# A graph-network layer on one core: VectorE adds chunk sums half by half, one-hots in between

## The reference

```python
msg = node_feat[src] + edge_feat                              # 400000 x 64
agg = jax.ops.segment_sum(msg, dst, num_segments=12500)       # sum of the messages of each node
h = jax.nn.relu(agg @ W1 + b1)                                # 64 -> 128
x = _layernorm(x + (h @ W2 + b2), axis=-1)                    # 128 -> 64
```

## Time and profile before

| | |
|---|---|
| median of 3 runs | 1467.95 us |
| profiled execution | 1467.16 us |
| its span, first to last instruction | 1465.4 us |
| mean granted TensorE clock | 0.906 |
| TensorE busy | 1223.0 us, 83% |
| VectorE busy | 1217.6 us, 83% |
| GpSimd busy | 967.6 us, 66% |
| ScalarE busy | 751.7 us, 51% |

### The profile page before, as it was taken

How to read it: one execution, slowest core, us unless ns; L and a number is a source line. 1 busy time by engine, 2 the same in 40 slices (tenths; PEclk the granted TensorE clock), 3 DMA queues, 4 the chain that set the end, 5 groups by cost and what they waited for, 6 DMA issues and landing times.

```text
span 1465.4 us, 47112 instructions
## 1 busy us (share of the span) xinstructions
PE 1223.0 (83%) x18748; PEld 1107.5 (76%) x18749; DVE 1217.6 (83%) x2696; ACT 751.7 (51%) x941; POOL 967.6 (66%) x1043
## 2 busy tenths in 40 slices
PE   1457878888888899888989899999999999999873
PEld 1356777776778888887878889888888888898642
DVE  5499888898988898989998888888889899887333
ACT  3734322233445455554455666666666666665252
POOL 6767777777676677777767667676666766674132
PEclk8566698899998999999999999999999999999975
DMA  6724444444443444444443434444333444332132
GB/s 166 177 77 126 114 128 117 113 128 121 110 120 104 117 114 120 112 123 109 105 127 105 119 102 107 117 108 110 108 104 103 123 113 111 101 100 64 33 76 67
DMA packets 157980, 161.09 MB, mean 110 GB/s; under 512 B 52803, under 2 KB 141955, under 8 KB 157427
## 3 DMA queue, kind: packets, MB, share of 16 engines
q1 hardware_dynamic: 126149, 123.61, 28.6%
q0 software_dynamic: 31616, 34.50, 12.4%
HBM read 153.06 MB, written 4.93 MB: 108 GB/s over the span
## 4 chain that ended last, share of the span: by engine, by line
PE 44%; DVE 28%; issue 17%; DVEq 5%; ACT 3%; DMA 2%; POOL 1%; POOLq 0%; SPq 0%
PE sums_ps L1175 20%; PE counted_ps L1158 12%; DVE oh_key L953 11%; PE chunk_ps L1140 10%; DVE oh_lo L949 8%; DVEq L907 3%; ACT counts L741 3%; DVE lists L918 2%; DVE onehot L893 2%; DMA lists<-in_dst 1%; DVEq L918 1%; POOL x_parts L658 1%; DVE less_b L843 1%; DMA edge_records<-counts 1%; PE turn_ps L1186 1%
## 5 line engine op out<-in xcount | busy, mean ns | idle before, releaser
L617 POOL DMA_INDIRECT xmsg<-in_x,idx_t x925 | 888.4, 960 | 292.4 <-issue 275.0
L741 ACT CAST counts<-counted_ps 128x784 bf16<-128x784 f32 (+2 forms) x728 | 618.3, 865 | 500.8 <-PE counted_ps L1158 494.3
L1158 PE MATMUL counted_ps<-oh_key,oh_lo 128*128 128x98 bf16 (+1 forms) x5264 | 579.4, 232 | 143.6 <-DVE oh_key L953 109.5
L1175 PE MATMUL sums_ps<-x_parts,counts 128*128 128x193 bf16 (+3 forms) x4900 | 629.0, 254 | 0.3
L1158 PEld LDWEIGHTS counted_ps<-oh_key,oh_lo 128*128 128x128 bf16 x5264 | 381.8, 103 | 204.8 <-DVE oh_key L953 149.9
L949 DVE TENSOR_TENSOR oh_lo<-chunk_ps,tables 128x768 bf16<-128x768 f16 (+3 forms) x622 | 444.6, 715 | 94.6 <-PE counted_ps L1158 57.8
L953 DVE TENSOR_TENSOR oh_key<-chunk_ps,tables 128x1176 bf16<-128x1176 f16 (+2 forms) x622 | 459.5, 739 | 0.0
L1175 PEld LDWEIGHTS sums_ps<-x_parts,counts 128*128 128x128 bf16 (+3 forms) x4900 | 455.8, 118 | 4.6 <-issue 3.1
L1140 PE MATMUL chunk_ps<-onehot,cmsg 128*64 128x16 f32 (+4 forms) x4400 | 167.3, 222 | 6.3 <-DVE lists L918 5.3
L1140 PEld LDWEIGHTS chunk_ps<-onehot,cmsg 128*64 128x64 f32 x4400 | 153.6, 147 | 22.6 <-issue 9.5
L918 DVE TENSOR_TENSOR lists<-lists,chunk_ps 64x48 f32 (+6 forms) x625 | 113.8, 182 | 30.5 <-PE chunk_ps L1140 8.4
(11 more groups left out here) (104 smaller groups left out, 459.6 us busy)
## 6 DMA issues: line engine op xcount, KB each, us to landing
cmsg<-in_edge_attr SPq DMA_DIRECT2D x440, 160.0 KB
gmsg<-in_edge_attr SPq DMA_DIRECT2D x185, 160.0 KB
xmsg<-in_x,idx_t POOLq DMA_INDIRECT x925
x_parts<-in_x SPq DMA_DIRECT2D x12, 256.0 KB, 3.2
out_nodes<-x_parts SPq DMA_DIRECT2D x12, 256.0 KB, 2.6
edge_records<-counts SPq DMA_DIRECT2D x1, 1500.0 KB
lists<-in_src SPq DMA_DIRECT2D x1, 1400.0 KB
lists<-in_dst SPq DMA_DIRECT2D x1, 1400.0 KB
```

The lines of the kernel that those rows point to most:

```text
L617: pool.indirect_dma_start(xmsg[:, at * D:(at + 1) * D], None, x, bass.IndirectOffsetOnAxis(ap=idx_t[:, of:of + 1], axis=0)).then_inc(gathe ...
L741: nc.scalar.copy(to.rearrange("p h (m n) -> p h m n", m=m), ps.rearrange("p m (n h) -> p h m n", h=HI)).then_inc(unit_kept, 1)
L1158: mm = nc.tensor.matmul(unit_ps[u][:, col:col + slot.key_cols], oh_lo[s % RING][:, n * P:(n + 1) * P], oh_key[s % RING][:, n * slot.key_co ...
L1175: mm = nc.tensor.matmul(sums_ps[0:n, 0:XC], counts[b % 2][:, h * P:h * P + n], x_parts[:, h * XC:(h + 1) * XC], start=(h == 0), stop=(h == ...
```

## The change

The four adds of a visit are reordered, and a pair's one-hots go between two adds of one half. With places p0 to p3 of a visit, VectorE issued before: add p0 (half 0), p1 (half 1), p2 (half 0), p3 (half 1), one-hots A, one-hots B, register load. It now issues: add p0 (half 0), one-hots A, add p2 (half 0), add p1 (half 1), one-hots B, add p3 (half 1), register load. `ADDED` is numbered in the new order. `LAG` is 4, so the `range` steps are what they were.

```diff
+        def in_halves(places):
+
+            return places[0::2] + places[1::2]
+
         ADDED = {}
         half_of = lambda key: key[1] % 2 if key[0] == "chunk" else 0
         for s in range(NS + 1):
-            for place, _, _ in JOBS_AT[s]:
-                if place >= LAG:
-                    ADDED["chunk", place - LAG] = len(ADDED) + 1
+            for q in range(0, len(JOBS_AT[s]), LAG):
+                for place in in_halves([place for place, _, _ in JOBS_AT[s][q:q + LAG]]):
+                    if place >= LAG:
+                        ADDED["chunk", place - LAG] = len(ADDED) + 1
...
             for s in range(NS + 1):
-                for q in range(0, len(JOBS_AT[s]), 4):
-                    quad = JOBS_AT[s][q:q + 4]
-                    for place, _, _ in quad:
+                for q in range(0, len(JOBS_AT[s]), LAG):
+                    quad = JOBS_AT[s][q:q + LAG]
+                    for k, place in enumerate(in_halves([place for place, _, _ in quad])):
                         if place >= LAG:
                             add(place - LAG)
-                    for k in range(0, len(quad), 2):
-                        mark(quad[k:k + 2])
+                        if k % 2 == 0:
+                            mark(quad[k:k + 2])
                     load_offsets(quad)
```

## The result

The changed kernel takes 1517.09 us (median of 4 runs, 1515.84 to 1517.89), the kernel before 1468.13 us beside it (4 runs): 1.0332 times as long, 95% interval 1.0314 to 1.0350. That is 49 us more. I had forecast 25 more and a range up to 1512; the time is that of the rival called "all of it passes" (1517). The two conditions are kept apart.

A forecast was written before the change was run, and what follows sets the result against it. VectorE was taken to set the pace from 60 to 260 us (93% of the chain), with varying shares later. Its 49.5 us extra, weighted by chain shares, gave 23.8, plus 1: 25 on 1467.16, 1492 us; range 1474 to 1512.

The forecast's parts named there:

- all of it passes: Rival: VectorE's whole extra reaches the end, because TensorE's later start takes away the slack; +50, 1517 us; chance 0.11.
- The load's place: VectorE's sequencer: load stands behind p3's wait, so oh_lo comes 0.35 us later for short one-hots A, A - 0.06 for longer.
- VectorE's extra: Later oh_lo summed over the visits of the slot loop: 49.5 us on VectorE.
- The order by itself worth nearly nothing: Visits without a load: oh_lo 0.02 us earlier for long A, 0.15 later for the 80-column one.
- The gaps: Between VectorE instructions: next starts 0.08 us before the last one's end on the same half, 0.03 after where it changes.
- What passes: Extra of each slot-loop stretch times VectorE's side's share of the chain: 23.8 us reach the end.
- allowed 1 us for such shifts: Slot loop: later VectorE takes over parts of the chain that are TensorE's; 1 us added, making 25.
- TensorE's release at 0: Products of a visit wait for p3, 0.2 us later in the visit shown; taken as hidden, 0 us.
- 57.8 us of idle time end with TensorE: VectorE's idle time before oh_lo, cited for the absorbed rival as more than the 49.5 us that come.
- absorbed: Rival: VectorE's lead of up to three slots swallows the later oh_lo; +9, 1476 us; chance 0.13.
- Signs in the profile: First three stretches: idle before oh_lo rises from 56 us by 25 to 30, named issue; between adds 22 to a few.

The follow-up runs named there:

- load_late_b: Kernel before, its order kept, only the register load held back by a wait on VectorE's sequencer: 1480.39 us against 1467.82, ratio 1.0083.
- pe_late_b: Kernel before, only TensorE's first products of a visit wait for both pairs' one-hots: 1474.58 us, ratio 1.0040.
- before_load_slot: Kernel before with the register load moved behind the slot's oh_lo and oh_key: ratio 0.9945, where the kernel before took 2394 us.

## Why the prediction was wrong

- **The load's place: right.** The load starts 1.20 us into the visit on average instead of 0.78; in the visit shown `oh_lo` is later by 0.34 us, forecast 0.35. p3's wait (737.65) stands on the sequencer and the load (737.85) behind it.
- **VectorE's extra: right.** 47.4 us, forecast 49.5.
- **The order by itself worth nearly nothing on VectorE: right.** Visits without a load 1.76 to 1.77 us. The gaps are the forecast ones: one-hots A start 0.07 us before p0's end (154.86 against 154.93), and B 0.04 after p1's. The Trainium skill's rule on operands that begin in another quadrant ("VectorE: DVE Perf Modes", section on two Vector instructions with no wait between them) held in the new order too; this trace agrees.
- **What passes: wrong, and this is the step that failed.** "I multiply by the share of the chain that is VectorE's side" gave 23.8 of 49.5 us, plus 1. The held-back load alone passed by 0.88 (0.68 to 1.03), which makes some 42 us of the 47.4. From 867 us on, with VectorE on 13% of the chain, 0.6 of it passed there, and in the changed kernel 14.8 us against 18.7 of extra; less the up to 4.2 us of TensorE's later start in that part this is 0.6 again. The chain of one execution says who was last in it. It does not say by how much the other was early: VectorE was busy for 432 of 482 us in that part. I had the busy time in the page's slices (8 or 9 tenths in most) and used the chain instead.
- **The chain's shares themselves moved.** I had expected VectorE's share to rise between 260 and 860 us and allowed 1 us for such shifts. The chain of the changed kernel from 582 to 901 us, then from 901 to 1398:

```profile
by line: PE sums_ps L1180 22.1%; issue 18.0%; DVE oh_key L958 14.5%; PE counted_ps L1163 13.0%; PE chunk_ps L1145 9.8%; DVE oh_lo L954 9.3%; DVEq L912 3.1%; DVE lists L923 2.0%; DVE less_b L848 1.4%; DVEq L923 1.4%; DVE sums L935 0.8%; DVE 
by line: PE sums_ps L1180 30.4%; PE counted_ps L1163 17.4%; PE chunk_ps L1145 12.7%; issue 11.1%; DVE oh_key L958 9.7%; DVE oh_lo L954 3.4%; DVEq L912 3.2%; ACT counts L746 3.1%; DVE lists L923 1.9%; PE turn_ps L1191 1.1%; DVE less_b L848 1
```

  TensorE's lines have 45% in the first of them, where TensorE and ScalarE together had 26% between 560 and 860 us, and with ScalarE 65% in the second, where they had 87%. So VectorE's share fell in the middle and rose to as much as 35% at the end. Shares that one change of 3% moves by 20 points are no price for a delay.
- **Slack.** VectorE's idle time directly before `oh_lo` and directly behind `oh_key`, which has no load in it, was 0.0, 7.6 and 18.5 us in the three parts before. What passed of the held-back load falls in the same order (all, 0.9, 0.6). That the shortage of slack is why so much passed is argued from this and was not tested by itself; in the changed kernel that idle time is 0.5, 9.2 and 17.5 us, so it was not simply used up. The runs show only how much passes.
- **The rival that has the right time.** "All of it passes" had it because TensorE's later start takes away the slack. With TensorE's release unchanged 0.88 passed, and the release alone cost 6 to 7 us. Its 50 us for VectorE alone and the 49 measured agree in the number and not in what makes it up.
- **TensorE's release at 0: wrong, small.** It costs 6 to 7 us by itself (3.8 to 7.9 by the interval). I had it as hidden, from one visit where the products end together with `oh_key`.
- **"57.8 us of idle time end with TensorE" was misread.** The group before `oh_lo` now has 86.5 us put down to TensorE:

```profile
L954 DVE TENSOR_TENSOR oh_lo<-chunk_ps,tables 128x768 bf16<-128x768 f16 (+3 forms) x622 | 445.1, 716 | 141.8 <-PE counted_ps L1163 86.5
```

  Yet idle time before `oh_lo` that follows directly on `oh_key`, and so has no load before it, is 26 us before and 27 after. The remainder of the 57.8 and of the 86.5 lies behind adds and one-hots: it is nearly all the load's time, named after the semaphore that `oh_lo` also waits for. So the slack that spoke for "absorbed" was less than half of what I read.
- **Signs in the profile.** The idle time before `oh_lo` of the first three stretches rose from 56 to 86 us, as forecast, but not under the name of issue, which has 42 of it (31 before). The idle time between adds did not fall to a few: the adds' group on the page has 27.5 us before it, 8.3 of them for TensorE, against 30.5 and 8.4. Little of it was stalls between the adds of a visit (0.11 us in the visit of the earlier trace rows).
- **The clock.** TensorE's granted clock is lower in all three parts (0.82 to 0.76, 0.93 to 0.89, 1.00 to 0.98), and its busy time 16.5, 16.8 and 6.0 us longer. Its two levels are 1.2 and 2.4 GHz, so this is a larger share of time at the lower one; TensorE also waited more for the adds. TensorE's busy time in the three parts rose with each of the two edits too, by 8 us in load_late_b and 13 in pe_late_b. Whether it adds to the loss or only fills time that TensorE had is open; no run separates it.

## What to carry to other kernels

In this kernel a register load of 1.2 us on VectorE's sequencer was covered only by the work that had been handed over before it. Moving a waiting instruction ahead of such a load takes cover away, even when no engine instruction is added: 0.42 us per visit with one load here. An engine's share of the chain did not tell how much of its extra time reaches the end; look at its idle time that truly waits for others, stretch by stretch. Where VectorE and TensorE were both busy for nine tenths, 0.6 of the extra passed, and more where VectorE had no such idle time. Put the load where the most work has just been handed over, here behind the slot's one-hots; that version was faster than the kernel before by 0.4 to 0.55%, measured only where the kernel before took 2400 us.

## What the runs showed of the hardware

The same kernel took 1468 us or about 2400 us in different sessions; one chip gave both within three hours. In the long ones the stretch ahead of the first slot takes as long as before (60 to 61 us against 63) and the loss is spread over the slot loop. Engines that wait for TensorE often start well after its recorded ends there. From before_load_slot, TensorE's counting and ScalarE's copy that waits for it:

```profile
130.34 0.71 PE L1160 MATMUL counted_ps<-oh_key,oh_lo 128*128 128x98 bf16 x12 [0.83 <-DVE oh_key L953]
...
131.41 0.53 PE L1160 MATMUL counted_ps<-oh_key,oh_lo 128*128 128x98 bf16 x8 [0.36 <-issue]
...
133.10 0.98 ACT L741 CAST counts<-counted_ps 128x980 bf16<-128x980 f32 x1 [6.13 <-PE counted_ps L1160]
```

The last counting matmul is recorded as ended at 131.94, and the copy starts 1.16 us later. Of the copies that ScalarE waited for by over 0.3 us, 149 of 426 start over 0.5 us after the last counting record that ended ahead of them, up to 11.8 us; in the trace of before none of 287 starts over 0.04 us after it. The mean granted clock was 0.73 instead of 0.91. The cause was not found, and in that condition most of a change on VectorE does not show in the time.
